# Group norm with patch top-k: image stored patch by patch, horizontal differences on GpSimd

## The reference

```python
s = W_GRAD * _grad_mag(x) + W_ACT * jnp.abs(x)          # x is the normalised image here
sp = s.reshape(n, C, nh, P, nw, P).mean(axis=(3, 5))    # P = 32
ranks = jnp.argsort(jnp.argsort(-sp, axis=1), axis=1)
mask = (ranks < k)                                       # k = C // 2
...
x = x + _L0_conv_ref(_gn(x))
```

## Time and profile before

| | |
|---|---|
| three runs | 2316.19, 2316.2 and 2318.4 us, median 2316.2 |
| profiled execution | span 2313.6 us from the first to the last instruction; the median run is 2.6 us longer |
| VectorE, ScalarE, TensorE, GpSimd busy | 89%, 71%, 69%, 1% of the span |
| DMA | 776.77 MB, 336 GB/s over the span |

### The profile page before, as it was taken

How to read it: one execution, slowest core, us unless ns; L and a number is a source line. 1 busy time by engine, 2 the same in 40 slices (tenths; PEclk the granted TensorE clock), 3 DMA queues, 4 the chain that set the end, 5 groups by cost and what they waited for, 6 DMA issues and landing times.

```text
span 2313.6 us, 22003 instructions
## 1 busy us (share of the span) xinstructions
PE 1596.0 (69%) x5960; PEld 952.8 (41%) x5960; DVE 2059.7 (89%) x3195; ACT 1647.5 (71%) x3007; POOL 16.5 (1%) x29
## 2 busy tenths in 40 slices
PE   6999999668877788648777888638887788700000
PEld 4555555434444445425444544425454444400000
DVE  8999999899999999999999999999999999993232
ACT  6999999479888889359888889539988888700000
POOL 0000000000000000000000000000000000000000
PEclk9999999879888889769888889769988888855555
DMA  6634453168999999688899999789899999599999
GB/s 291 255 145 181 181 217 147 73 274 330 382 412 406 397 407 387 269 340 354 351 407 406 403 404 387 277 340 369 340 405 410 399 408 404 214 372 432 432 431 392
DMA packets 41247, 776.77 MB, mean 336 GB/s; under 512 B 4576, under 2 KB 4576, under 8 KB 4576
## 3 DMA queue, kind: packets, MB, share of 16 engines
q1 hardware_dynamic: 41184, 775.96, 82.1%
HBM read 507.51 MB, written 268.44 MB: 335 GB/s over the span
## 4 chain that ended last, share of the span: by engine, by line
issue 87%; DMA 9%; DVE 2%; DVEq 1%; POOL 0%; SPq 0%; POOLq 0%; PE 0%
DMA out_dram<-ring 6%; DMA ring<-in_x_dram 3%; DVE ring L645 1%; DVEq L573 0%; DVE kept L645 0%; DVE largest L787 0%; DVE again L645 0%; POOL rstd L259 0%; DVE diff L792 0%; SPq L264 0%; DVE diff L749 0%; DVE coef L789 0%; DVE coef_now L636 0%; PE rank_bank L499 0%; DVEq L97 0%
## 5 line engine op out<-in xcount | busy, mean ns | idle before, releaser
L532 ACT ACTIVATE diff<-diff 128x1024 f32<-128x1024 f32 x669 | 697.8, 1044 | 306.3 <-DVE diff L609 202.7
L581 DVE BATCH_NORM_STATS2 stats<-ring 128x6 f32<-128x512 f32 x960 | 575.4, 679 | 5.7 <-DMA ring<-in_x_dram 5.7
L609 DVE TENSOR_TENSOR diff<-ring 128x2016 f32<-128x2016 f32 x240 | 539.8, 2270 | 1.5 <-ACT diff L532 1.5
L554 ACT ACTIVATE junk<-ring,record 128x1024 f32<-128x1024 f32 x480 | 531.0, 1106 | 7.0
L435 PE MATMUL vertical<-ring,plus 128*128 128x512 f32 x600 | 374.4, 709 | 60.3 <-ACT vertical L539 60.3
L645 DVE TENSOR_SCALAR again<-again,coef_now 128x512 f32<-128x512 f32 x752 | 349.2, 539 | 10.1 <-issue 5.4
L539 ACT ACTIVATE vertical<-vertical 128x1024 f32<-128x1024 f32 x320 | 321.1, 1003 | 47.2 <-PE vertical L412 46.8
L439 PE MATMUL vertical<-ring,plus 128*128 128x512 f32 x600 | 333.7, 638 | 0.0
L436 PE MATMUL vertical<-ring,minus 128*128 128x480 f32 x600 | 323.7, 624 | 0.0
L441 PE MATMUL vertical<-ring,minus 128*128 128x480 f32 x600 | 290.6, 566 | 0.0
L436 PEld LDWEIGHTS vertical<-ring,minus 128*128 128x128 f32 x600 | 128.6, 214 | 170.9 <-issue 170.9
(11 more groups left out here) (103 smaller groups left out, 1533.2 us busy)
## 6 DMA issues: line engine op xcount, KB each, us to landing
ring<-in_x_dram SPq DMA_DIRECT2D x66, 4096.0 KB, 22.8
again<-in_x_dram SPq DMA_DIRECT2D x94, 2048.0 KB, 13.1
out_dram<-again SPq DMA_DIRECT2D x94, 2048.0 KB, 8.5
out_dram<-ring SPq DMA_DIRECT2D x10, 4096.0 KB, 38.7
kept<-in_x_dram SPq DMA_DIRECT2D x7, 4096.0 KB, 23.6
out_dram<-kept SPq DMA_DIRECT2D x8, 2048.0 KB, 9.9
out_dram<-kept SPq DMA_DIRECT2D x3, 4096.0 KB, 32.9
ring<-in_x_dram SPq DMA_DIRECT2D x4, 1024.0 KB, 7.9
```

The source lines that it names most:

```text
L532: done = nc.scalar.activation(v, v, ACT.Abs, accum_out=sums[r][:, which, w:w + 1])
L554: done = nc.scalar.activation(junk[:], rows[:, :, n * PATCH:(n + 1) * PATCH], ACT.Abs, bias=record[r][:, 2:3], accum_out=sums[r][:, 2, n:n ...
L581: nc.vector.bn_stats(stats[:, k, :], buffer[:, k * BN:(k + 1) * BN])
L609: nc.vector.tensor_tensor(d[:, :, lo:hi], rows[:, :, left_col + lo + 1:left_col + hi + 1], rows[:, :, left_col + lo - 1:left_col + hi - 1] ...
```

## The change

The host now hands over the image patch by patch: a partition holds 8 patches of 32 x 32 pixels one behind the other, and the output has the same layout. Tiles, halves and DMA sizes stay as they were. GpSimd makes all horizontal differences: for each of four pairs of patches two or three operations for the columns at the patch edges, and one subtraction of 2 x 32 x 30 elements, into two `across` buffers. VectorE keeps the vertical differences of patches 5 to 7, now patch by patch into `down_ps` (PSUM) and `scratch`. ScalarE takes the absolute sums of all but the last pair (`across_sums` on VectorE takes pair 3, in image 0 pairs 2 and 3, and none in the first step after a ranking). In image 0 VectorE also sums one vertical patch (`down_sum`). So ScalarE has 19 sums per tile in image 0 and 22 in the steady steps of images 1 to 3. A half is finished in four operations of 1024 contiguous elements, not eight of 512, and reads `coef` directly. The statistics are cut in four parts with other work between them. Every step but the one after a ranking finishes two halves, the last step none, the ranking two.

```diff
-PIX = PATCH * WIDTH
+AREA = PATCH * PATCH
+PIX = COLS * AREA
...
+OUT_FIRST, OUT_LOOPED, OUT_LAST, OUT_RANKING = (0, 2, 2), (2, 2, 2), (2, 2, 2, 0), 2
+ORDER_FIRST = "a a d0 v0 a a h0 v1 a a v2 d2 h1 a v3 a v4".split()
+ORDER = "a a d0 v0 h0 a d1 v1 a h1 a v2 d2 a h2 v3 a a v4".split()
+ORDER_AFTER_RANKING = "a a d0 v0 h0 a a v1 h1 a a v2 h2 a a v3 h3 d1 d2 v4".split()
...
-        diff = [sb(f"diff{b}", [PARTS, PATCH, 2 * PATCH]) for b in range(3)]
+        across = [sb(f"across{b}", [PARTS, 2, PATCH, PATCH]) for b in range(2)]
+        scratch = sb("scratch", [PARTS, 3 * AREA // 2])
+        down_sb = scratch[:, 0:AREA].rearrange("p (r c) -> p r c", r=PATCH)
+        thrown = sb("thrown", [PARTS, AREA], BF16)
-        junk = pb("junk", [PARTS, PATCH, PATCH])
+        down_ps = pb("down_ps", [PARTS, PATCH, PATCH])
+        down = [down_ps[:], down_sb]
...
+            def differences(tile, buffer, r):
+                xs = by_patch(buffer)
+                nm = record[r][:, 2:3]
+                pool.wait_ge(minus_mean_ready, tile + 1)
+                for k in range(PAIRS):
+                    d = across[k % 2]
+                    w = 2 * k
+                    pool.wait_ge(across_free[k % 2], 2 * tile + k // 2 + CREDIT_ACROSS)
...
+                    nc.gpsimd.tensor_tensor(d[:, begin:2, :, 0], xs[:, w + begin:w + 2, :, 1],
+                                            xs[:, w + begin - 1:w + 1, :, PATCH - 1], ALU.subtract)
+                    nc.gpsimd.tensor_tensor(d[:, 0:end, :, PATCH - 1], xs[:, w + 1:w + 1 + end, :, 0],
+                                            xs[:, w:w + end, :, PATCH - 2], ALU.subtract)
...
+                    nc.gpsimd.tensor_tensor(d[:, :, :, 1:PATCH - 1], xs[:, w:w + 2, :, 2:PATCH],
+                                            xs[:, w:w + 2, :, 0:PATCH - 2], ALU.subtract)\
+                        .then_inc(across_ready, 1)
...
+            def wait_done_with(count):
+                sp.wait_ge(across_ready, PAIRS * count)
+                wait_analysed(sp, count)
...
-            def differences(tile, buffer, r, items):
+            def vertical_difference(tile, buffer, k):
+                dve.wait_ge(down_free[k % 2], (2 * tile + k // 2 if k % 2 == 0 else tile) + CREDIT_DOWN)
+                if k == 0:
+                    dve.wait_ge(halo_ready, tile + 1)
...
+            def across_sums(tile, r, k):
+                dve.wait_ge(across_ready, PAIRS * tile + k + 1)
+                nc.vector.tensor_reduce(sums[r][:, 0, 2 * k:2 * k + 2], across[k % 2][:], AX.XY, ALU.add,
+                                        apply_absolute_value=True).then_inc(across_free[k % 2], 1)
...
-                for w in range(COLS):
-                    v = rows[:, :, w * PATCH:(w + 1) * PATCH]
-                    done = nc.vector.tensor_scalar(v, v, coef_now[:, 0, w:w + 1], coef_now[:, 1, w:w + 1],
+                for j in range(HALF_COLS):
+                    v = pixels[:, j * AREA:(j + 1) * AREA]
+                    w = first + j
+                    done = nc.vector.tensor_scalar(v, v,
+                                                   coef[:, bass.ds(t, 1), 0, w:w + 1].rearrange("p a w -> p (a w)"),
...
+                own = [] if after_ranking else [2, 3] if first_image else [3]
...
+                settle()
+                if not (isinstance(g, int) and g == 0 and u == 0):
+                    vertical_difference(tile, buffer, 0)
+                vertical_difference(tile, buffer, 1)
+                if first_image:
+                    settle()
+                    down_sum(place)
+                next_statistics(0)
+                for w in halves[:1]:
+                    apply_again(image, g, w)
+                vertical_difference(tile, buffer, 2)
+                next_statistics(1)
+                for w in halves[1:]:
+                    apply_again(image, g, w)
...
+                next_statistics(2)
+                for k in own[-2:-1]:
+                    across_sums(tile, place, k)
+                next_statistics(3)
...
+                for k in own[-1:]:
+                    across_sums(tile, place, k)
+                if after is not None:
+                    minus_mean(tile + 1, after)
```

More of the change, by code:

```diff
@@ L48 @@
[L48 to L86, removed]
+REC = 3 + COLS
@@ L87, in output_plan @@
+def output_plan():
+    first, start = numbered(OUT_FIRST, 0)
+    looped, end = numbered(OUT_LOOPED, start - 2 * RING)
+    assert end == start - 2 * RING + sum(OUT_LOOPED) and sum(OUT_LOOPED) == 2 * RING
+    last, end = numbered(OUT_LAST, start - 2 * RING)
+    ranking = list(range(end, end + OUT_RANKING))
+    assert 2 * RING * (LOOPED - 1) + end + OUT_RANKING == HALVES
     return first, looped, last, ranking
-REC = 3 + COLS
 def groupnorm_patch_topk(nc: bass.Bass, x: bass.AP, out: bass.AP):
@@ L677, in step @@
                 place = RING if u == RING else u
-                early = EARLY_ITEMS if isinstance(g, int) and g == 0 and u == 0 else 0
-                at_start, in_middle, at_end = output
-                for w in at_start:
-                    output_half(image, g, w)
-                if not early:
-                    settle()
-                differences(tile, places[place], place, range(early, ITEMS))
-                if before is not None:
+                buffer = places[place]
+                first_image = isinstance(image, int) and image == 0
@@ L699, in step @@
-                if after is not None:
-                    statistics(tile + 1, places[after], after, place_loaded[after], count)
+                next_statistics(2)
+                for k in own[-2:-1]:
+                    across_sums(tile, place, k)
+                next_statistics(3)
                 if place == RING:
                     stable_variance(image)
-                for w in at_end:
-                    output_half(image, g, w)
+                elif before is not None:
+                    keep_record(tile - 1, before, RING * g + u - 1)
@@ L806, in rank @@
                 settle()
-            places = [*ring, kept]
+                if not last:
+                    apply_kept(0)
+                    apply_kept(1)
             place_loaded = [*ring_loaded, kept_loaded]
-            statistics(0, ring[0], 0, first_loaded, 1)
+            for part in range(4):
+                statistics(0, ring[0], 0, first_loaded, 1, part)
             minus_mean(0, 0)
             settle()
-            differences(0, ring[0], 0, range(EARLY_ITEMS))
+            vertical_difference(0, ring[0], 0)
             dve.wait_ge(constants, CONSTANTS)
```

432 lines of the change are left out of this document (208 added, 224 removed).

## The result

The changed kernel takes 2364.0 us (median of 4 runs, 2363.1 to 2365.8) against 2317.3 us of the kernel before (4 runs on the same chip, 2316.2 to 2318.8): ratio 1.020, interval 1.019 to 1.022. It is 2.0% slower. The forecast of 2273 us was wrong in its sign.

A forecast was written before the change was run, and what follows sets the result against it. VectorE and ScalarE were taken to bound image 0, VectorE and DMA the steady steps. 2313.6 + 14 (image 0) - 12 (first changeover) - 45 (images 1 to 3) = 2270.6, plus 2.6: 2273 us; own range 2235 to 2300, stretched 2230 to 2500.

The forecast's parts named there:

- I forecast from this row that VectorE isn't held for the length of a GpSimd operation: All tiles: finishing beside a GpSimd power took 3.73 us against 3.74 with GpSimd idle, so VectorE loses nothing, GpSimd a little.
- blocking (0.30): Rival, chance 0.30: VectorE and GpSimd each hold the other for a whole instruction; 13 us lost, 37.4 per steady step, 2575 total.
- the forecast (0.40): Main case, chance 0.40: no holding of VectorE, 2273 us, own range 2235 to 2300.
- Its turning point: In the blocking rival, a wide GpSimd subtraction of 3 us gives a step of about 32 us, no gain or loss.
- That is two bounds at once: Steady steps of the kernel before: VectorE (274.4 of 280 us) and DMA (share 0.99, 403 GB/s) both bound 31.1 us.
- The tail's 415 GB/s: Tail's DMA rate; if DMA reached it in images 1 to 3, an image is 485 + 18 and the total 2240, within the forecast.
- I take 2.2 ns, 4.2 us: GpSimd's wide subtraction of 1920 elements, bounded by 1.5 and 5.8 us; with small ones at 0.3, a tile is 20 us.
- The work of VectorE's step: Images 1 to 3: VectorE's steady step falls to 24.4 us against 31.1, under DMA's 31.
- the halo wait: Steady step: the first vertical difference waits for the halo, about 1.2 us behind the minus mean.
- The chain through pair 3: Image 0: pair 3 waits for the buffer freed after h1, then reduction and minus mean: 26.4 us against 25.5, +14 total.
- The first changeover: First change of images, not DMA's: VectorE loses some 22 us of work; as DMA also needs time, -12 taken.
- the tail's term of 0: Tail: it is DMA's, and the change doesn't touch its DMAs, so 0 us.

The follow-up runs named there:

- Experiment 8: A kernel of its own, not the changed one: eight VectorE operations of each kind beside an idle GpSimd, subtractions, MEMSETs or powers; 248.5 us in one run.
- Experiment 2: Changed kernel with the second input of VectorE's wide vertical subtraction a zero row in PSUM; GpSimd works in full: 2187.2 us, ratio 0.944 to the kernel before.
- experiment 3: Changed kernel with finishing in images 1 to 3 as scalar_tensor_tensor, one SBUF and one PSUM input, added coefficient left out: 2318.9 us, ratio 1.001 to the kernel before.
- experiment 1: Changed kernel with GpSimd making only one 32-element subtraction per pair and signalling, horizontal differences left out: 2102.6 us, ratio 0.907 to the kernel before.
- experiment 5: As experiment 1, plus a GpSimd MEMSET of 1922 elements behind each pair's small subtraction: 2116.2 us, ratio 0.913 to the kernel before.
- experiment 6: Kernel before the change, with halves finished in 4 operations of 1024 contiguous elements and not 8 of 512: 2246.6 us, ratio 0.969.
- experiment 4: Changed kernel with pair 3's reduction moved behind the minus mean, except in an image's last tile; nothing left out: 2248.8 us, ratio 0.972 to the kernel before.
- experiment 7: Experiments 3 and 4 together on the changed kernel, added coefficients computed into PSUM, nothing left out: 2234.9 us, ratio 0.964 to the kernel before.

## Why the prediction was wrong

**The step that decided and failed: "I forecast from this row that VectorE isn't held for the length of a GpSimd operation".** It is held. The row (eight finishing operations in 3.73 us beside a power of 3.15) showed a GpSimd operation with 16 elements, and the text said itself that "it says little of a long stream"; so it gave no reason to put blocking (0.30) under the forecast (0.40). Experiment 8 shows the holding by itself, a near sum of both times. Experiment 2, with the holding taken off the vertical differences alone, shows 177 us in the kernel, and experiments 2 and 3 that it hangs on the form of VectorE's instruction. The range of 2230 to 2500 holds the 2364 us only because it was stretched into this rival; the forecast's own, 2235 to 2300, does not. Against the sum, image 0 is 13 us longer, the rest of the analysis up to image 3's last tile 79 longer, and the tail as forecast.

**The blocking rival had the mechanism and a wrong price.** It foresaw four meetings with wide subtractions and 13 us lost per step; there were four, and 8.5 us. The subtraction is 3.4 us and not 4.2, and the meetings cost 2.25, 1.28, 3.07 and 1.78 us in the step shown where 3.6, 2.0, 4.3 and 2.1 were foreseen. So 37.4 us per step became 32.45, and 2575 us became 2364. Its turning point, "With a wide subtraction of 3 us the step is about 32 and the case is even", was near: at 3.4 us the step is 32.45 and the kernel 2% slower. No run has one of 3 us.

**"That is two bounds at once" was wrong.** A DMA share of 0.99 at 403 GB/s was not a full rate: shares of 0.99 to 1.01 stood beside anything from 403 to 431 GB/s. The same 12.58 MB went in 29.2 us in experiments 1 and 5, and with VectorE's 1.5 us less the kernel before went to 29.6 (experiment 6). The tail's 415 GB/s stood in the same group and said as much; it was counted as a side case. This error alone made the forecast too high and not too low: with the vertical differences not held the kernel is at 2187, and without GpSimd's work at 2103, both under 2273. With DMA at 29.2 us a step there would have been 1.9 us to save in every steady step.

**GpSimd's price.** "I take 2.2 ns, 4.2 us": measured 3.39 us where nothing disturbs it, 1.77 ns an element, inside the bounds of 1.5 and 5.8 us. The estimate from the Trainium skill's figure (GPSIMD Engine Reference, section "Performance versus the Vector engine"), also 4.2 us, was as high. The small ones have 0.30 to 0.44 us, not 0.3, and means of 0.8 to 0.9 with holding. In the steady step shown GpSimd is busy 20.7 us, and 21.8 from its first operation to its last, against 20; so the two errors nearly cancel.

**The work of VectorE's step** was right: 24.4 us forecast, 24.0 without the losses. In it the halo wait was under-sized, 2.1 us and not 1.2, and the overlaps between instructions made up for it.

**Image 0.** The chain through pair 3 was right, and experiments 2 and 4 show it; 26.4 was forecast, and 27.1 came in most steps, as the reader sees in this one, which starts with the minus mean at 156.36 (VectorE, then GpSimd's pair 3, then TensorE's first matmuls and two of ScalarE's sums):

```profile
175.61 2.47 DVE L582 BATCH_NORM_STATS2 stats<-ring 128x6 f32<-128x512 f32 x4
178.15 0.59 DVE L585 BATCH_NORM_AGGREGATE record<-stats 128x2 f32<-128x96 f32 x1
178.66 2.60 DVE L618 TENSOR_SCALAR records<-record 128x3 f32 x1
...
181.27 2.29 DVE L613 TENSOR_REDUCE sums<-across 128x2 f32<-128x2048 f32 x1
183.47 0.15 DVE L589 TENSOR_SCALAR record<-small_bank 128x1 f32<-128x1 f32 x1
```

```profile
176.84 0.43 POOL L262 TENSOR_TENSOR across<-ring 128x64 f32<-128x64 f32 x1 [3.47 <-ACT across L545]
...
177.83 3.40 POOL L271 TENSOR_TENSOR across<-ring 128x1920 f32<-128x1920 f32 x1
```

```profile
157.53 1.55 PE L448 MATMUL vertical<-ring,plus 128*128 128x512 f32 x2
158.88 1.81 PE L449 MATMUL vertical<-ring,minus 128*128 128x480 f32 x2
```

```profile
172.53 1.00 ACT L539 ACTIVATE vertical<-vertical 128x1024 f32<-128x1024 f32 x1
...
175.63 1.04 ACT L545 ACTIVATE across<-across 128x1024 f32<-128x1024 f32 x1
```

The aggregate is done at 178.7; but the copy is held until L271 ends at 181.2, and the reduction stands behind both, so the minus mean comes 4.7 us after the aggregate. The forecast's error lies earlier: ScalarE is done with h1, whose buffer pair 3 needs, 20.4 us after the minus mean and not 18.4. TensorE's third patch comes 15.6 us after it and not 13.9, because the first takes 5.9 us and not 4.24: its first matmuls take 1.55 and 1.81 us where later ones take 1.10 and 0.97. TensorE had been idle for 3.1 us before, and the granted clock is 0.78 on the mean of 156.4 to 164 and 1.00 from 164 to 183. Pair 3 (4.4 us against 5.1) and what follows it (2.2 against 2.6) were shorter than forecast.

**The ends of an image and the tail.** The first changeover was forecast 12 us shorter and is 12.5 shorter (66.1 to 53.6); the tail's term of 0 was right (-0.4). What the prediction didn't see is that four steps an image had been short, 27.4 to 28.1 us, because they finished one half of a tile; with two halves and the holding they take 32.45.

**What stays open.** Experiment 8 does not tell whether the power holds nothing because it reads so little or because it computes between its accesses. Nor is there a run in which GpSimd only reads, or one that shows why image 0 took 7 us more in experiment 7.

## What to carry to other kernels

In these runs work moved to GpSimd is free for VectorE only beside statistics, reductions and two-input instructions with one input in PSUM. Beside subtractions with both inputs in SBUF or the fast two-scalar form it costs nearly its own duration again (18.06 and 14.93 us for eight, against 8.61 and 5.87), so each VectorE instruction that will overlap should first be put in a form that isn't held (second input from PSUM, even at 1.27 us against 0.81), and the fast form kept where GpSimd idles. A row is evidence only for operations that move as much as the one it is read for. A DMA share of 1.0 is no bound until a rate has been seen to stay there with the engines waiting for it. A reduction that nobody waits for belongs behind the instruction that starts the next tile: experiment 4 gained 115 us by it.

## What the runs showed of the hardware

- A VectorE copy of three elements is held as long as a large one (0.76 us for eight alone, 10.14 beside subtractions).
- GpSimd's writing alone holds the two-scalar finishing (5.87 to 12.91 us for eight) but not the two-input subtraction (8.61 to 8.63).
- A power of 16 elements takes GpSimd 2.9 us and doesn't hold VectorE (5.87 us for eight finishing operations beside it and alone).
- With the second input in PSUM, a two-input operation runs beside GpSimd at full speed (9.62 us for eight alone, 9.61 beside it).
- DMA shares of 0.99, 1.00 and 1.01 stood for 403, 420 and 431 GB/s; VectorE waited for DMA at 431 alone (26 of 146 us).
